# A Mamba layer with a mixture of experts: block ends on GpSimd, another order of states, and 16 scan units written out

## The reference

```
xz = x @ in_proj_w.T + in_proj_b;  x_in, z = split(xz)            # 512 channels each
x_conv = silu(causal conv over 4 tokens (x_in) + conv_b)
dt_low, B, C = split(x_conv @ x_proj_w.T)                         # 64, 16, 16
dt = softplus(dt_low @ dt_proj_w.T + dt_proj_b);  A = -exp(A_log)
for each token, channel d, state s:
    A_bar = exp(dt * A);  B_bar = (A_bar - 1) / A * B
    h = A_bar * h + B_bar * x_conv;   y = sum_s h * C + D * x_conv
x1 = layernorm(x + (y * silu(z)) @ out_proj_w.T + out_proj_b)
out = layernorm(x1 + shared_mlp(x1) + weighted sum of the 2 best of 16 experts(x1))
```

## Time and profile before

| | us |
|---|---|
| median of 3 runs | 3115.8 (3113.47 to 3116.19) |
| profiled execution, its own time | 3113.81 |
| its span | 3112.0 |
| TensorE, VectorE busy | 2706.1, 2468.0 |
| GpSimd, ScalarE busy | 2368.1, 1818.1 |

### The profile page before, as it was taken

How to read it: one execution, slowest core, us unless ns; L and a number is a source line. 1 busy time by engine, 2 the same in 40 slices (tenths; PEclk the granted TensorE clock), 3 DMA queues, 4 the chain that set the end, 5 groups by cost and what they waited for, 6 DMA issues and landing times. The chain is left out here.

```text
span 3112.0 us, 45581 instructions
## 1 busy us (share of the span) xinstructions
PE 2706.1 (87%) x9762; PEld 1546.9 (50%) x9763; DVE 2468.0 (79%) x3915; ACT 1818.1 (58%) x3580; POOL 2368.1 (76%) x2077
## 2 busy tenths in 40 slices
PE   7989898988989898989898989888998988499986
PEld 3445454444545454545454545444544545377743
DVE  5988888888788878888888788887888898266644
ACT  6575757566757575656657575757565744123246
POOL 2988887878788878888888788887878788355542
PEclk8999999999989999999898999999998979699998
DMA  3333333333333333333333323333333332765564
GB/s 85 105 98 111 90 109 100 111 92 101 100 103 97 101 98 111 100 103 106 100 98 97 106 89 115 93 111 92 111 95 98 98 98 93 197 188 178 174 194 158
DMA packets 250558, 350.10 MB, mean 113 GB/s; under 512 B 77863, under 2 KB 125483, under 8 KB 249772
## 3 DMA queue, kind: packets, MB, share of 16 engines
q1 hardware_dynamic: 234684, 302.34, 33.0%
q0 software_dynamic: 15600, 44.79, 4.1%
HBM read 288.59 MB, written 58.45 MB: 112 GB/s over the span
## 5 line engine op out<-in xcount | busy, mean ns | idle before, releaser
L638 POOL TENSOR_TENSOR hc<-h,c_rep 128x512 f32<-128x512 f32 x896 | 1138.5, 1276 | 358.4 <-DVE h L1172 170.7
L969 PE MATMUL y_ps<-hc,dg_inv 128*128 128x512 f32 x1792 | 961.0, 624 | 33.4 <-POOL hc L638 22.2
L630 POOL TENSOR_TENSOR h<-x_conv,b_rep 128x512 f32<-128x512 f32 x640 | 829.5, 1296 | 2.3 <-ACT carry L734 2.3
L720 ACT ACTIVATE a_ps<-dt,a_mat 128x512 f32<-128x512 f32 x640 | 439.8, 687 | 669.1 <-DVE h L1172 632.9
L1172 DVE TENSOR_TENSOR_SCAN h<-a_ps,carry,h 128x512 f32<-128x512 f32 x640 | 807.0, 1271 | 24.4 <-DVE skip L1208 7.6
L985 PEld LDWEIGHTS g_ps<-b_steps,x_conv_rows 128*128 128x128 f32 x3072 | 448.6, 213 | 320.9 <-issue 176.1
L969 PEld LDWEIGHTS y_ps<-hc,dg_inv 128*128 128x128 f32 x1792 | 328.5, 196 | 429.9 <-issue 305.2
L985 PE MATMUL g_ps<-b_steps,x_conv_rows 128*128 128x128 f32 x3072 | 460.3, 298 | 86.0 <-DVE carry L1188 85.9
L1141 DVE SCALAR_TENSOR_TENSOR h<-a_ps,h 128x512 f32<-128x512 f32 x640 | 428.4, 669 | 59.4 <-ACT a_ps L720 58.1
L1180 DVE TENSOR_TENSOR_SCAN h<-g_ps,carry,h 128x512 f32<-128x512 f32 x256 | 327.3, 1278 | 30.3 <-DVE g_ps L1165 25.8
L1038 PE MATMUL work<-x_in,dg_tap 128*128 128x512 f32 x512 | 271.8, 618 | 48.9 <-DVE x_tok L1233 48.9
(11 more groups left out here) (250 smaller groups left out, 3821.1 us busy)
## 6 DMA issues: line engine op xcount, KB each, us to landing
c_rep<-bc_rows SPq DMA_DIRECT2D x512, 256.0 KB, 3.3
b_rep<-bc_rows SPq DMA_DIRECT2D x320, 256.0 KB, 3.7
gathered<-slot_rows SPq DMA_DIRECT2D x144, 129.5 KB
gathered<-y_planes SPq DMA_DIRECT2D x32, 512.0 KB, 5.7
x_t<-in_x_t SPq DMA_DIRECT2D x16, 512.0 KB, 4.9
x_tok<-in_x_tok SPq DMA_DIRECT2D x16, 512.0 KB, 3.8
out<-mixed_rows SPq DMA_DIRECT2D x16, 512.0 KB, 3.1
x_t_rows<-y_gated SPq DMA_DIRECT2D x15, 512.0 KB, 5.0
```

Of the source, the lines that this page charges most:

```text
L630: nc.gpsimd.tensor_tensor(h[:, i % SLOTS, e], x_conv[:, u[1] % 2, chunk(i, e)], b_rep[:, n % BS], ALU.mult).then_inc(u_ready, 1)
L638: nc.gpsimd.tensor_tensor(hc[:, i % 2, e], h[:, i % SLOTS, e], c_rep[:, i % CS], ALU.mult).then_inc(hc_pool, 1)
L720: nc.scalar.activation(out, dt[:, c], ACT.Exp, scale=a_mat[:, c, s:s + 1]).then_inc(made, 1)
L969: nc.tensor.matmul(y_ps[:, e], by, hc[:, i % 2, e], start=first_one, stop=(i % HALF == HALF - 1)).then_inc(summed, 1)
```

## The change

The order of kinds becomes `ddfdfddfdfdddfdf`, with still 10 plain and 6 factored states in each half, and three of them (4, 9 and 15) are multiplied with C by VectorE in place of two. All places of the woven work are given anew, those of `make_u`, `make_a` and `make_du` now one by one. B rows are loaded for pair i+6. `find_ends` and `make_both` go from VectorE to GpSimd, with the sign made by ScalarE (`turn_ends`). A softplus step covers both chunks of a group at once. The logits' bias is added by one matmul, and their four groups go to four items. The norm's sums are at items 20 and 22; the last scatter is at item 14, and SyncE reloads `x_tok` at pair `SCATTER_AT[-1] // 2 + 1`, now 8. The store of `x1_t` stays at pair 16. The units are written out. `b_high` and `b_mid` are gone from the split of the bias at the start, which now works in place.

```
-LOGS = 4 * FACTORS
+LOGS = 2 * FACTORS
...
+HCS = 2
+LAG = 2
+B_LEAD = 6
...
-KINDS = "ddfddfdfddfddfdf"
-BY_VECTOR = (2, 10)
+KINDS = "ddfdfddfdfdddfdf"
+BY_VECTOR = (4, 9, 15)
...
-        PLACE = [("d2", 0), ("d3", 1), ("x0", 2), ("x1", 4), ("o0", 6), ("o1", 10), ("c0", 14), ("c1", 18), ("r0", 22), ("r1", 23),
-                 ("x2", 24), ("x3", 26), ("t0", 28), ("t1", 29), ("T2", 30), ("T3", 31), ("c2", 32), ("c3", 36), ("lg", 40),
-                 ("z2", 41), ("low", 43), ("bc", 48), ("d0", 49), ("d1", 50), ("pf", 51), ("z3", 52), ("z0", 54), ("z1", 56),
-                 ("T0", 58), ("T1", 59), ("r2", 60), ("r3", 61)]
+        PLACE = [("x0", 0), ("d3", 2), ("d2", 3), ("x1", 4), ("c0", 5), ("c1", 8), ("T2", 13), ("T3", 14), ("o0", 14), ("o1",
+                 18), ("x2", 20), ("r0", 23), ("r1", 27), ("c2", 29), ("x3", 30), ("c3", 35), ("r2", 38), ("t1", 39), ("t0", 39),
+                 ("r3", 40), ("lg", 40), ("low", 42), ("d0", 46), ("bc", 46), ("d1", 48), ("z1", 51), ("z2", 52), ("pf", 53),
+                 ("z3", 56), ("z0", 56), ("T1", 59), ("T0", 60)]
+        U_AT = [-5, -2, None, 4, None, 6, 8, None, 12, None, 15, 18, 20, None, 26, None, 29, 32, None, 34, None, 38, 41, None,
+                45, None, 47, 50, 51, None, 55, None]
+        A_AT = [-1, 1, 3, 4, 5, 7, 10, 12, 11, 13, 16, 18, 22, 20, 24, 25, 28, 31, 31, 36, 38, 39, 41, 42, 46, 45, 48, 53, 55,
+                56, 57, 58]
+        DU_AT = [None, None, 3, None, 5, None, None, 12, None, 14, None, None, None, 23, None, 29, None, None, 33, None, 37,
+                 None, None, 43, None, 47, None, None, None, 57, None, 59]
+        SCATTER_AT = (1, 2, 3, 5, 9, 10, 12, 14)
+        ADD_RELU_AT = (59, 60, 18, 20)
+        Z_AT = (49, 5)
+        STEPS_AT = (47, 48, 53, 55, 58, 63)
+        SUMS_AT = (20, 22)
+        SILU_AT = (15, 43)
+        SQUARES_AT = ((52, 53, 54), (5, 6, 13))
+        LOGS_AT = ((53, 57), (12, 16))
+        TURN_AT, ENDS_AT, BOTH_AT = 52, 61, 50
+        MAX_AT, INDEX_AT, IDS_AT, CHOOSE_AT, CANDIDATES_AT, REDUCE_AT, PLACES_AT, NOTED_AT = 45, 47, 49, 52, 55, 60, 61, 63
+        ROOT_AT, INVERSE_AT, NORMALISE_AT = 24, 26, 28
+        GATE_AT, HALO_IN_AT, HALO_OUT_AT = 58, 4, 47
+        SKIP_AT = (26, 29, 39, 41)
...
-            with eng.Fori(0, (UNITS - 2) // 2) as j:
-                unit_program((j, 1), inner)
-                unit_program((j, 2), inner)
+            for k in range(1, UNITS - 1):
+                unit_program((0, k), inner)
...
-        SCATTER_AT = (1, 2, 3, 4, 8, 9, 10, 11)
...
-                    nu, ni = after(u, i, 4)
+                    nu, ni = after(u, i, B_LEAD)
                     if plain(ni) and not (plan is last and nu != u):
                         load_b(nu, ni)
...
                     if i == 16 and plan is not second:
-                        emptied_all(sp, plan, u, ["t1"])
+                        emptied_all(sp, plan, u, [max("t0", "t1", key=ORDER.get)])
                         sp.dma_start(d["x1_t"][number(later(u, -1))], x1_t).then_inc(x1_t_out, 16)
...
+            def make_both(u, plan):
+
+                n = later(u)
+                pool.wait_ge(parts_in, count(n, 32, 32))
+                if plan is not first:
+                    emptied_all(pool, plan, u, [max("r2", "r3", key=ORDER.get)])
+                nc.gpsimd.tensor_tensor(both[0:NF], b_part[:], c_part[:], ALU.mult).then_inc(both_ready, 1)
+
+            def find_ends(u):
...
+                pool.wait_ge(ends_turned, count(n, 1, 1))
...
+                for c in range(CH):
+                    one = nc.gpsimd.tensor_tensor(minus_u[:, nq, c], b_minus[:], last_of[:, c].unsqueeze(1).to_broadcast([P, NF, TT]),
+                                                  ALU.mult)
+                one.then_inc(ends_ready, 1)
...
+            def turn_ends(u):
+
+                n = later(u)
+                act.wait_ge(ends_in, count(n, 16, 16))
+                wait(act, ends_ready, count(n, 1, 0))
+                nc.scalar.activation(b_minus[:], b_end[:, :, :, 1], ACT.Copy, scale=-1.0).then_inc(ends_turned, 1)
...
+                    logits = work[:, bank, 0:TT * NE].rearrange("p (t e) -> p t e", e=NE)
+                    if part == 0:
+                        emptied_all(pe, plan, u, ["t0", "t1"])
+                        nc.tensor.matmul(logits, ones[:], b_gate[:].unsqueeze(1).to_broadcast([1, TT, NE]), start=True, stop=False)
+                    for k in range(KT):
+                        mm = nc.tensor.matmul(logits[:, part], x1_t[:, k, part * P:(part + 1) * P], w_gate[:, k],
+                                              start=False, stop=(part == TT - 1 and k == KT - 1))
...
-                nc.vector.scalar_tensor_tensor(out=poly[:, half], in0=factor[:, half], scalar=ATANH[k][2], in1=other[:, half],
+                nc.vector.scalar_tensor_tensor(out=poly[:], in0=factor[:], scalar=ATANH[k][2], in1=other[:],
                                                op0=ALU.add, op1=ALU.mult).then_inc(softplus_step, 1)
...
-                    if m in (12, 16):
-                        norm_sums(u, plan, f"o{(m - 12) // 4}")
-                    if m == 22:
+                    if m in SUMS_AT:
+                        norm_sums(u, plan, f"o{SUMS_AT.index(m)}")
+                    if m == INVERSE_AT:
                         normalise(later(u, -1))
```

More of the change, by code:

```diff
@@ L546, in _ @@
             load_parts((0, -1))
-            for i in range(4):
+            for i in range(B_LEAD):
                 if i < 2:
@@ L617, in scatter @@
                 r, tt = divmod(n, TT)
+                if n == 0:
+                    first_columns(u)
+                    pool.wait_ge(columns, count(later(u, -1), COLUMNS, 7))
+                elif n == TT:
+                    second_columns(u)
+                    pool.wait_ge(columns, count(later(u, -1), COLUMNS, 9))
                 nc.gpsimd.indirect_dma_start(d["x_rows"], bass.IndirectOffsetOnAxis(kept.place[:, r, tt:tt + 1], 0),
@@ L628, in make_u, with u_s_at @@
                     ou, oi = before(u, i, SLOTS)
-                    slot_free(pool, ou, oi)
+                    if on_pool(oi):
+                        carried_wait(pool, ou, oi)
+                ou, oi = before(u, i, SLOTS)
+                if on_pool(oi):
+                    hc_wait(pool, ou, oi, e)
+                else:
+                    wait(pool, scanned, count(ou, ITEMS, 2 * oi + e + 1))
                 nc.gpsimd.tensor_tensor(h[:, i % SLOTS, e], x_conv[:, u[1] % 2, chunk(i, e)], b_rep[:, n % BS],
                                         ALU.mult).then_inc(u_ready, 1)
+            U_PLACE = sorted((U_AT[i] + e, i, e) for i in range(PAIRS) for e in range(2) if plain(i))
+            def u_s_at(u, plan, m):
+                for at, i, e in U_PLACE:
+                    if at == m:
+                        make_u(u, i, e)
+                    if at == m - ITEMS and plan is not last:
+                        make_u(later(u), i, e)
             def make_hc(u, i, e):
@@ L647, in unit_program @@
                     i, e = divmod(m, 2)
-                    if plan is not second and m == SCATTER_AT[0]:
-                        pool.wait_ge(columns, count(later(u, -1), COLUMNS, 7))
-                    if plan is not second and m == SCATTER_AT[TT]:
-                        pool.wait_ge(columns, count(later(u, -1), COLUMNS, 9))
                     if plan is not second and m in (IDS_AT, PLACES_AT):
                         pool.wait_ge(route, count(later(u, -1), ROUTE, 2 if m == IDS_AT else 7))
-                    if plan is not second and m == PLACES_SEEN:
+                    if plan is not second and m == NOTED_AT:
                         pool.wait_ge(route, count(later(u, -1), ROUTE, ROUTE))
@@ L658, in unit_program @@
                         make_hc(pu, pi, e)
-                    nu, ni = after(u, i, 2)
-                    if plain(ni) and not (plan is last and nu != u):
-                        make_u(nu, ni, e)
+                    u_s_at(u, plan, m)
                     if plan is not second and m == IDS_AT:
@@ L821, in squared @@
             def squared(n, g, k):
[L823 removed]
+                wait(act, softplus_step, count(n, LOGS, g * FACTORS))
                 if k == 0:
@@ L886, in weave @@
                         tile(u, plan, t)
-                if plan.has("c0") and m in (26, 42):
-                    half = 0 if m == 26 else 2
+                if plan.has("c0") and m in SILU_AT:
+                    half = 2 * SILU_AT.index(m)
                     emptied_all(act, plan, u, [f"c{c}" for c in (half, half + 1)])
@@ L923, in unit_program @@
                         halo_wait(u, plan, m)
+                    if plan.has("pf") and m == NOTED_AT:
+                        act.wait_ge(route, count(later(u, -1), ROUTE, ROUTE))
                     a_s_at(u, plan, m)
@@ L1071, in weave @@
                     tile(u, plan, t, part)
```

(17 more changed lines are left out.)

171 lines of the change are left out of this document (70 added, 101 removed).

## The result

The changed kernel takes 3006.2 us (median of 4 runs, 3003.4 to 3010.6) against 3116.0 (4 runs, 3113.5 to 3118.6): ratio 0.965 [0.963, 0.967], 110 us less. 2910 was forecast. The profiled execution took 3003.4 us.

What follows compares the result with a forecast made beforehand. Order and waits set the 163.9 us unit, VectorE leading. Terms of -5.6-6.0-5+3 = -13.6 us for 14 inner units (-190), with ends and branch -206, gave 2910 us; forecast 2850 to 2990, range 2815 to 3065.

Steps and rivals of the forecast that it cites:

- rival B: TensorE, busy 146.6 us a unit, becomes the bound and keeps most of its idle time: 3044 us, chance 0.22.
- Reload, -5.6: Norm's sums at items 20 and 22: VectorE's wait for reloaded token rows goes, -5.6 us a unit (-5.6 to 0).
- VectorE's work, -6.0: Block ends and `both` leave VectorE, softplus steps merge, a third state is added: -6.0 us a unit (-8 to -2).
- TensorE, -1: Same matmuls, but the logits' bias goes in once and their groups are spread: -1 us of work a unit.
- Join and exponential waits, -5: VectorE's waits for TensorE's joins and ScalarE's exponentials fall from 13.7 to about 8.7 us a unit (-13 to +6).
- Store hold, +3 (0 to +10): SyncE stands 23 us at the x1_t store, delaying C and B loads; GpSimd idles 6 to 8: +3 us a unit.
- No loop, -3 (-32 to 0): Written-out units save the backward branches, 5.4 us each on TensorE, 0.06 on other engines: -3 us in all.
- Ends of the stage: First and last scan units, priced apart: first -6 us, last -8, and +1 before the first scan.
- signs that were named for a right forecast: No token-row wait, GpSimd block ends 0.2 to 0.5 us, unit near 150, softplus below 2, no TensorE branches, hold signs.
- Rival D: Scatters end late at items 9 to 14, so the reload isn't early: 2990 us, counted with the forecast's upper side.
- A: The waits go nearly all, since no busy engine exceeds 147 us a unit: about 2790 us, chance 0.17.
- Rival C: Slower: the store holds SyncE and GpSimd becomes the bound at 169.3 us a unit: about 3190 us, chance 0.08.

Runs made afterwards that it cites:

- reload_late: softplus_later with the reload of the token rows issued at pair 10 instead of 8: 3023.2 us, ratio 0.972 to the kernel before.
- softplus_later: store_later with the softplus step of item 16 moved to 23 and GpSimd's adds of items 18 and 20 to 25 and 26: 2917.0 us, ratio 0.937.
- before_written_out: The kernel before with its fourteen inner units written out and nothing else changed: 3112.8 us, ratio 1.000.
- loop_back: The changed kernel with the loop over two units put back, GpSimd's column steps one item earlier: 3060.9 us, ratio 0.981 to the kernel before.
- store_later: The changed kernel with the store of x1_t at pair 21 in place of 16: 2934.0 us, ratio 0.942 to the kernel before.
- token_rows_alone: The kernel before with the first half of each unit's token rows loaded at pair 16 of the unit before: 3109.6 us, ratio 0.998.
- all_but_order: The kernel before, written out, block ends and `both` on GpSimd, half the token rows loaded a unit ahead, sign turned within `b_end`: 3060.4 us, ratio 0.984.
- ends_on_gpsimd: The kernel before, loop kept, with block ends and `both` on GpSimd and their sign on ScalarE: 3111.2 us, ratio 0.998.

## Why the prediction was right or wrong

The time lies in the range and the sign was right. The gain was half of that forecast: an inner unit lost 7.8 us, not 13.6. 3006 us lies outside the 2850 to 2990 that the forecast's own sum had been given, and nearer to rival B's 3044 than to 2910. The range held it because it was wide enough to take in B's 3044.

- **Reload, -5.6: the wait went as forecast** (-5.5). Its worth depends on the rest: nothing in the kernel before, all of it (reload_late) in softplus_later. The bound of 0, "if VectorE only waits elsewhere", was real.
- **VectorE's work, -6.0: mis-sized.** It was -3.8. Block ends, `both` and the third state came as computed (hc 109.8/12.3 = 8.9 us against 5.9, carries +0.8). The merged softplus saved 0.6, not 2.8: I gave each step one wait of 0.6 us, and one step in four waits 4.3. The four-element operation `spread` fell from 0.91 to 0.16 us, which was in no term.
- **GpSimd, 133.0:** measured 1590.7/12 = 132.6.
- **TensorE, -1: right for the work, and the clock was left out.** Its busy time fell by 6.2 us. With each busy stretch multiplied by its granted clock it is 135.3 us before and 134.1 after, -1.2; the other 5.0 is what the low clock no longer adds (11.0 us before, 6.0 after). I had the low clock only behind the branch. It is also there ahead of the join of item 42, the "cause" in the earlier trace rows, and adds up to 3 us to that stretch.
- **Join and exponential waits, -5:** 13.7 to (61.1+67.4)/12.3 = 10.4, so -3.3: joins -5.2, exponentials +1.8. Beside them 7.7 us of other waits came up: `y_ps`, score, C rows, B factors. The sum had put them at nothing, apart from the hold's +3.
- **Store hold, +3 (0 to +10): the mechanism as told**, silence 20.8 us for 23, GpSimd idle 8.7 for 6 to 8, C rows late on VectorE. Its size was 5.3.
- **No loop, -3 (-32 to 0): failed.** In size it was right for the kernel before (before_written_out, 0). But the change moved the work that covered VectorE's branch, and with that the loop costs 55 us (51 by the ratios), half of the whole gain. The step that failed was "the backward branch costs SyncE, GpSimd, ScalarE and VectorE 0.06 us": that is the branch's row, not the time to the next instruction. (The rows of these four engines are 0.04 to 0.06 us, about half of the 108 ns that the prediction has them agree with.) The Trainium skill (Runtime: NRT & Kernel Launch, "Instruction fetch mechanics") lets a taken branch outside the fetched pages wait for a fetch; I held the other engines against it, and loop_back's 5.5 us on VectorE agree with it. That the fetch is the cause no row shows. It cost the forecast nothing only because the loop went too, and that is luck. The join's wait of the earlier trace rows that the prediction called fixed (1.8 us a unit and more) went with the loop as well: all such gaps are 2.8 us a unit before and 0.4 after.
- **Ends of the stage:** first unit -6.1 (forecast -6); last +1.5 (-8); the first scan came 5.7 us later (+1), but it lies between 63.2 and 66.6 us in the kernels of one start-up code, so that part is not settled. The last unit has the store's hold too, which the forecast left out there: without it (store_later) it takes 141.8 us, -3.7.

Of the signs that were named for a right forecast, the token rows, the block ends on GpSimd and those of the hold came. A unit near 150 us did not, and of the four softplus steps one took 5.5 us.

Rival D did not come, nor A. Rival C's mechanism was there (8.7 us of GpSimd's idle time), but GpSimd had room. Of rival B this is true: in items 10 to 52 of the unit shown TensorE is busy 94% of the time in the kernel before and 96% in before_written_out, and the joins there wait for it. That this is why single parts gave nothing and the whole 110 us is argued: no run speeds up TensorE alone, and in token_rows_alone 2.6 of the 4 us went to one VectorE operation behind GpSimd. The order of states, with the merged softplus and new placements, is worth all_but_order less the changed kernel, 54 us (59 by the ratios); which of them stays open, but the join waits are shorter by 8 us a unit there (13.2 against 5.0).

## What to carry to other kernels

Price an edit together with what the removed work had covered: the same loop cost 0 us in one kernel and 55 in the other. The same wait of some 6 us a unit on VectorE was worth nothing where TensorE and GpSimd were full behind it, and 7 us in softplus_later; a test is to put the wait back into the better kernel. When producers of a store move later, move the store on its queue as well: here that one number was worth 72 us.

## What the runs showed of the hardware

- A taken branch's row says 0.06 us on VectorE, while its next instruction starts 3.2 us later or more in ends_on_gpsimd and 4.1 to 5.6 us later in loop_back.
- A VectorE operation with two SBUF inputs behind a busy GpSimd can wait for more than the running instruction: one of four elements a lane took 3.64 us (0.16 in the changed kernel), one of 1024 columns 5.52 (1.22 for the same size elsewhere). The Trainium skill (SBUF — State Buffer, section "SBUF: two separate sides") has the two exclude each other for a whole instruction; these rows agree, and show that several GpSimd instructions can pass first.
- TensorE's granted clock adds to a late join: the stretch of item 42 in the kernel before lasts 4.4 us at 1.00 and 7.4 to 7.5 at 0.54. But a join can be late at full clock too: 3.3 us against 1.6 for the stretch of item 50, at 1.00 in both kernels.
